# Layer norms of the block preparation moved to ScalarE and GpSimd, with a step table for each engine

## The chip, the cores and the metric

One NeuronCore of a Trainium2 chip runs the whole kernel. The metric is the device time of one execution in microseconds (us); it is given as the median of three runs. Five engines work in parallel and meet only through semaphores: TensorE (PE, matmuls; PEld is its weight load), VectorE (DVE), ScalarE (ACT), GpSimd (POOL) and SyncE (SP), which issues the DMAs.

## The reference

The input x is 8 sequences of 512 tokens with 128 features. One layer is computed, cut here to what matters:

```
xn  = layernorm(x)                                # eps 1e-5
a   = softmax(q k^T / 8) v Wo + bo                # 16 heads of 64, q, k, v from xn
y   = xn + a
x2  = x + (y - mean(y)) * rsqrt(var(y) + 1e-3) * gamma + beta
f   = layernorm(x2)                               # eps 1e-5
s   = sigmoid(f @ router_w.T)                     # 64 experts in 8 groups
coef = top-4 groups, then top-8 experts, normalized, * 2.5     # one row of 64 per token
out = x2 + sum_e coef_e * (silu(f Wg_e) * (f Wu_e)) Wd_e + shared expert(f)
```

The two layer norms that the change is about are the one that gives x2 and the one that gives f.

## The kernel before

**Two phases.** First comes attention, in 64 pairs of heads (8 pairs for each of the 8 sequences), each pair in 4 slots; it ends near 800 us of the span. Then the experts: 8 blocks (one for each sequence of 512 tokens) of 33 tiles. Tile 0 is the shared expert, tiles 1 to 32 are two routed experts each. In both phases the high and low 16-bit halves of the operands are multiplied in three matmuls (`product`, `mm` at L998).

**One tile of the expert phase.** TensorE makes the gate (3 matmuls of 512 columns), the up projection (3), the spread coefficients (1) and the down projection (3). It works four tiles ahead: in its step k it issues gate, up and coefficients of tile k+4 (`gate_up`), then the down projection of tile k (`down`). The gate goes to ScalarE (`silu`, L628), then VectorE multiplies it with the up result (L957, "prod") and that with the coefficients (L963, "hid"), ScalarE takes the high half of it (L633, `hid_hi_tile`) and GpSimd the low half (L497, `hid_lo`). Gate, up and coefficients have two PSUM banks each. So the gate of tile t+2 waits for the silu of tile t, its up projection for the product (L957) of tile t, and its coefficients for the L963 of tile t.

**The preparation of the next block** runs among the tiles of the current one, in numbered steps. The function `route(m, r, k)` of each engine holds its part of step k; before the change step k is placed at tile k on every engine, behind the tile's own work. What is done:

- step 1, VectorE: y = xn + bias (L777); step 2: statistics (`bn_stats`, L781); step 3: mean and variance (`bn_aggr`, L785) and var + eps (L788)
- step 3, GpSimd: the power -0.5 of that (L435); step 2, GpSimd: x + beta (L446)
- step 4, VectorE: (y - mean) * gamma in four instructions (L792); step 6, VectorE: times 1/std, plus x, in four (L800), which gives x2
- steps 7 and 8: the same statistics of x2; step 9, VectorE: (x2 - mean) / std in four (L807), which gives f
- step 8, TensorE: four transposes of f (L1056); step 11, ScalarE, and 12, VectorE (L812): high and low half of the transpose; step 11, TensorE: the logits; step 14, ScalarE: the sigmoid (L563), which needs another activation table, so two table loads stand around it; step 14, GpSimd: scores plus bias (L441)
- steps 16 to 28, VectorE: the choice of groups and experts in small instructions that each read the one before (L822 to L887); step 27, TensorE: the transpose of the coefficients; step 30, ScalarE, and 31, VectorE: their halves

**Block 0** has no block ahead of it. Its preparation is placed by tables (`DVE_0`, `POOL_0`, `ACT_0`, `PE_0`) in the last 8 pairs of attention: slot 0 is slot 0 of pair 56, slot 31 the last slot of pair 63. `ROUTE_0` is 56.

Within an engine the order is as it is written out; nothing is reordered. On VectorE `own` counts an instruction, `settled` waits until all counted ones are done, and `then` does both.

Of the kernel before, what the change touches and what calls it, by code (L numbers as in the profile page):

```python
# [18 lines left out]
P = 128  # L19
# [45 lines left out]
def layer(nc, x, Wq, bq, Wk, bk, Wv, bv, Wo, bo, gamma, beta, router_w, e_bias,  # L65
          Wg, Wu, Wd, SWg, SWu, SWd, out):
    with ExitStack() as ctx:
# [74 lines left out]
        veps, rstd, total, share = (take(QT) for _ in range(4))  # L142
# [85 lines left out]
        xbeta = sem("xbeta")  # L228
        rstd_done = sem("rstd_done")
        c_var = sem("c_var")  # L230
# [161 lines left out]
        def _(pool):  # L392
# [29 lines left out]
            def route(m, r, k):  # L422
# [95 lines left out]
        def _(act):  # L518
# [38 lines left out]
            def route(m, r, k):  # L557
                if k == 11:
                    act.wait_ge(tr_c, m + 1)
                    nc.scalar.activation(fT_hi[r], bank_c(m), ACT.Copy).then_inc(tr_c_hi, 1)  # L560
# [79 lines left out]
            def run_block(n, r, last):  # L640
                for k in range(1, TILES if last else TILES + 1):
# [6 lines left out]
                    if not last:  # L648
                        route(n + 1, 1 - r, k)
# [9 lines left out]
        def _(dve):  # L659
# [92 lines left out]
            def route(m, r, k):  # L752
# [26 lines left out]
                if k in (2, 7):  # L779
                    for t in range(QT):  # L780
                        own(nc.vector.bn_stats(bn[:, t, :], (ya if k == 2 else x2[r])[:, t, :]))  # L781
                    settled()
                if k in (3, 8):
                    for t in range(QT):
                        own(nc.vector.bn_aggr(mean_var[:, t, :], bn[:, t, :]))  # L785
                    settled()
                    eps = POST_EPS if k == 3 else LN_EPS
                    nc.vector.tensor_scalar(veps, mean_var[:, :, 1], eps, None, ALU.add).then_inc(c_var, 1)  # L788

                if k == 4:  # L790
                    for t in range(QT):
                        own(nc.vector.scalar_tensor_tensor(out=ya[:, t, :], in0=ya[:, t, :], scalar=mean_var[:, t, 0:1],  # L792
                                                           in1=gamma_b, op0=ALU.subtract, op1=ALU.mult))
                if k == 6:
                    settled()
                    dve.wait_ge(rstd_done, m * 2 + 1)
                    dve.wait_ge(xbeta, m + 1)
                    wait(dve, out_sent, (m - 1) * 16)
                    for t in range(QT):
                        own(nc.vector.scalar_tensor_tensor(out=x2[r][:, t, :], in0=ya[:, t, :], scalar=rstd[:, t:t + 1],  # L800
                                                           in1=xin[r][:, t, :], op0=ALU.mult, op1=ALU.add))
                    settled()
                if k == 9:
                    dve.wait_ge(rstd_done, m * 2 + 2)
                    wait(dve, tr_c, m)
                    for t in range(QT):
                        last = nc.vector.tensor_scalar(xf[:, t, :], x2[r][:, t, :], mean_var[:, t, 0:1],  # L807
                                                       rstd[:, t:t + 1], ALU.subtract, ALU.mult)
                    last.then_inc(xf_done, 1)
# [167 lines left out]
            def run_block(n, r, last):  # L977
                for k in range(1, TILES if last else TILES + 1):
# [7 lines left out]
                    if not last:  # L986
                        route(n + 1, 1 - r, k)
# [8 lines left out]
        def _(pe):  # L996
# [51 lines left out]
            def route(m, r, k):  # L1048
                if k == 8:
                    pe.wait_ge(xf_done, m + 1)  # L1050
                    if isinstance(m, int) and m == 0:
                        pe.wait_ge(v_lo_done, ROUTE_0 + 3)
# [5 lines left out]
                if k == 11:  # L1058
                    pe.wait_ge(tr_c_lo, m + 1)
                    if isinstance(m, int) and m == 0:  # L1060
                        pe.wait_ge(v_lo_done, ROUTE_0 + 4)
# [219 lines left out]
```

## Time and profile before

| | |
|---|---|
| median of 3 runs (lowest, highest) | 1426.02 us (1425.08, 1428.25) |
| the profiled execution, its own time | 1428.47 us |
| its span, first to last instruction | 1426.7 us |
| TensorE busy (share of the span) | 1358.8 us (95%) |
| VectorE | 1119.4 us (78%) |
| ScalarE | 847.6 us (59%) |
| GpSimd | 888.0 us (62%) |
| granted TensorE clock, mean | 0.997 of full |

The span is what the trace shows between the first and the last instruction; the execution's own time is 1.8 us more. Shares are averages over both phases. TensorE's busy time is modelled from the start of pipelined matmuls, so its idle time is better read from the waits.

### The profile page before, as it was taken

How to read it: one execution, taken by the hardware profiler on the slowest of the kernel's cores; microseconds unless marked ns; L12 is line 12 of the kernel's file. 1: busy time of each engine (PE TensorE's matmuls, PEld its weight loads, DVE VectorE, ACT ScalarE, POOL GpSimd, SP SyncE). 2: the span in 40 equal slices, each digit the busy share in tenths (PEclk: the TensorE clock that was granted, in tenths of full speed). 3: DMA queues.
4: the chain of work that ended last, by engine and by line, in shares of the span. 5: the costliest groups of instructions: out<-in, count | busy, mean ns of one | idle time of the engine just before them, and what ended most of it. 6: DMA issues, size and time to landing. Idle time of an engine off the chain costs nothing.

```text
span 1426.7 us, 35687 instructions
## 1 busy us (share of the span) xinstructions
PE 1358.8 (95%) x12985; PEld 769.2 (54%) x12985; DVE 1119.4 (78%) x2005; ACT 847.6 (59%) x1496; POOL 888.0 (62%) x650
## 2 busy tenths in 40 slices
PE   3799999999999999999998999999989999999998
PEld 1366666666666666666665544344434444343443
DVE  5777777777777877777898888787878787777865
ACT  3566666666666666666666555555546554555554
POOL 3576777777677767767766755555555555555554
PEclk9999999999999999999999999999999999999999
DMA  7233333333333333333322000000000000000000
GB/s 181 52 76 84 78 85 75 82 79 74 79 74 79 74 79 74 83 78 84 86 62 51 9 1 8 8 8 9 2 15 0 15 0 16 0 15 0 1 8 8
DMA packets 84832, 67.45 MB, mean 47 GB/s; under 512 B 27792, under 2 KB 75216, under 8 KB 84688
## 3 DMA queue, kind: packets, MB, share of 16 engines
q1 hardware_dynamic: 84688, 65.52, 18.6%
q8 instruction: 92, 1.51, 0.5%
q14 instruction: 52, 0.43, 0.1%
HBM read 13.05 MB, written 2.10 MB: 11 GB/s over the span
## 4 chain that ended last, share of the span: by engine, by line
PE 63%; issue 19%; DVE 8%; POOL 5%; SPq 2%; ACT 1%; POOLq 0%; DMA 0%; DVEq 0%; ACTq 0%
PE bank L998 61%; POOL arena L497 4%; PE bank L1185 2%; DVE arena L902 1%; DVE arena L957 1%; DVE arena L963 1%; DVE arena L792 1%; POOL arena L462 1%; DVE arena L742 0%; DVE arena L807 0%; POOL arena L435 0%; DMA arena<-arena 0%; DVE arena L922 0%; ACT arena L633 0%; SPq L323 0%
## 5 line engine op out<-in xcount | busy, mean ns | idle before, releaser
L998 PE MATMUL bank<-arena 128*128 128x512 f16 (+5 forms) x12600 | 1328.0, 265 | 52.5 <-DVE arena L957 16.9
L998 PEld LDWEIGHTS bank<-arena 128*128 128x128 f16 (+3 forms) x12600 | 724.7, 98 | 622.0 <-issue 38.0
L462 POOL TENSOR_TENSOR arena<-arena 128x1024 f16<-128x1024 f32 x256 | 484.9, 1895 | 223.8 <-ACT arena L590 220.1
L497 POOL TENSOR_TENSOR arena<-arena 128x512 f16<-128x512 f32 x264 | 307.2, 1165 | 281.5 <-ACT arena L633 278.8
L902 DVE TENSOR_REDUCE arena<-bank 128x2 f32<-128x1024 f32 x256 | 311.8, 1218 | 55.2 <-PE bank L998 51.9
L590 ACT ACTIVATE arena<-bank 128x512 f32<-128x512 f32 x512 | 276.7, 595 | 82.7 <-PE bank L998 82.7
L633 ACT ACTIVATE arena<-arena 128x512 f16<-128x512 f32 x264 | 165.9, 628 | 189.9 <-DVE arena L963 186.5
L957 DVE TENSOR_TENSOR arena<-arena,bank 128x512 f32<-128x512 f32 x256 | 174.9, 683 | 88.8 <-ACT arena L628 59.0
L963 DVE TENSOR_TENSOR arena<-arena,bank 128x512 f32<-128x512 f32 x256 | 175.9, 687 | 29.3 <-DVE arena L957 3.8
L628 ACT ACTIVATE arena<-bank 128x512 f32<-128x512 f32 x264 | 155.5, 589 | 63.3 <-PE bank L998 62.7
L579 ACT ACTIVATE arena<-bank,arena 128x512 f16<-128x512 f32 x128 | 88.0, 688 | 152.8 <-PE bank L998 152.8
L933 DVE SCALAR_TENSOR_TENSOR arena<-bank,arena 128x512 f16<-128x512 f32 x128 | 95.4, 746 | 17.8 <-ACT arena L579 16.4
L939 DVE TENSOR_TENSOR arena<-bank,arena 128x512 f16<-128x512 f32 x64 | 44.2, 691 | 47.3 <-ACT arena L609 47.3
L594 ACT ACTIVATE arena<-bank 2x1024 f16<-2x1024 f32 x64 | 65.0, 1015 | 24.2 <-PE bank L998 24.1
L922 DVE TENSOR_TENSOR arena<-bank,arena 128x256 f32<-128x256 f32 x128 | 54.3, 424 | 4.4
L920 DVE RECIPROCAL arena<-bank 128x4 f32<-128x4 f32 x128 | 23.3, 182 | 35.4 <-PE bank L998 34.2
L615 ACT ACTIVATE arena<-bank 128x512 f16<-128x512 f32 x64 | 37.8, 590 | 11.9 <-PE bank L1185 11.8
L911 DVE TENSOR_TENSOR arena<-bank,arena 128x512 f32 (+1 forms) x64 | 43.6, 681 | 0.0
L928 DVE TENSOR_TENSOR arena<-bank,arena 128x512 f16<-128x512 f32 x64 | 43.5, 680 | 0.0
L1185 PE MATMUL bank<-arena 128*128 128x128 f32 x256 | 39.2, 276 | 2.4 <-DVE arena L911 2.3
L1185 PEld LDWEIGHTS bank<-arena 128*128 128x128 f32 x256 | 31.9, 143 | 15.5 <-DVE arena L911 4.3
L609 ACT ACTIVATE arena<-bank 128x512 f16<-128x512 f32 x64 | 38.4, 600 | 3.0 <-PE bank L998 1.4
(103 smaller groups left out, 416.8 us busy)
## 6 DMA issues: line engine op xcount, KB each, us to landing
arena<-arena SPq DMA_DIRECT2D x384, 128.0 KB, 2.4
arena<-in_L_attn_x SPq DMA_DIRECT2D x9, 256.0 KB, 2.9
arena<-in_L_ffn_Wg SPq DMA_DIRECT2D x32, 64.0 KB, 2.1
arena<-in_L_ffn_Wu SPq DMA_DIRECT2D x32, 64.0 KB, 2.2
arena<-in_L_ffn_Wd SPq DMA_DIRECT2D x32, 64.0 KB, 2.4
out<-arena SPq DMA_DIRECT2D x8, 256.0 KB, 2.3
arena<-in_L_attn_Wq SPq DMA_DIRECT2D x1, 512.0 KB, 4.1
arena<-in_L_attn_Wk SPq DMA_DIRECT2D x1, 512.0 KB, 5.1
```

The source lines that it names most:

```text
L462: pool.tensor_tensor(num_lo[:, u % 2, s, :, :], num[:, u % 2, s, :, :], num_hi[:, u % 2, s, :, :, 1], ALU.subtract).then_inc(lo_pool, 1)
L497: pool.tensor_tensor(hid_lo[:, r, :], hid[:, r, :], hid_hi[:, r, :], ALU.subtract).then_inc(hid_lo_done, 1)
L579: nc.scalar.activation(flat[:, (u + 3) % 2, (ZQH, ZKH)[which], :], ps_proj, ACT.Identity, bias=bias[:, n:n + 1]).then_inc(qk_hi, 1)
L590: nc.scalar.activation(num[:, u % 2, s, h, :], ps_st[ST_BANK[2 * s + h]], ACT.Exp).then_inc(exp_done, 1)
L628: nc.scalar.activation(silu_g[:, r % 3, :], ps_gate[r % 2], ACT.Silu).then_inc(silu_done, 1)
L633: nc.scalar.activation(hid_hi[:, r, :], hid[:, r, :], ACT.Copy).then_inc(hid_hi_done, 1)
L902: nc.vector.tensor_reduce(rmax[:, up % 2, q, :], ps_max2.rearrange("p (h k) -> p h k", h=2), AX.X, ALU.max).then_inc(max_done, 1)
L933: nc.vector.scalar_tensor_tensor(out=flat[:, (u + 3) % 2, (ZQL, ZKL)[s], :], in0=ps_proj, scalar=(bq8, bk_c)[s][:, n:n + 1], in1=flat[:, ( ...
L957: nc.vector.tensor_tensor(prod[:, i % 2, :], silu_g[:, i % 3, :], ps_up[i % 2], ALU.mult).then_inc(prod_done, 1)
L963: nc.vector.tensor_tensor(hid[:, i % 6, :], prod[:, i % 2, :], ps_coef[(k - 1) % 2], ALU.mult).then_inc(hid_done, 1)
L998: return nc.tensor.matmul(out_, lhsT, rhs, start=start, stop=stop, skip_group_check=True)
L1185: last = nc.tensor.transpose(ps_turn[:, k * P:(k + 1) * P], ctxn[:, u % 2, k, :], ident)
```

## The change

Steps 4 and 6 and step 9 leave VectorE:

- VectorE computes in steps 3 and 8 one more small row, the negated mean. GpSimd multiplies it with 1/std ("shift"), so that the norm is y * rstd + shift.
- ScalarE applies scale and shift, four instructions of 128 columns for each norm, in two steps: 4 and 5 for the first norm, 9 and 10 for the second.
- GpSimd multiplies with gamma and adds x + beta (new step 6, two instructions of 128x512). VectorE waits for its result before step 7.

Every engine gets a table for blocks 1 to 7 too (`DVE_N`, `POOL_N`, `ACT_N`, `PE_N`), which says at which tile its steps stand. Steps 16 to 28 of VectorE, before at tiles 16 to 28, now stand at tiles 19 to 28, so that three tiles hold two steps each. On GpSimd the preparation's steps now stand ahead of the tile's own instruction, not behind it.

```diff
-DVE_0 = {0: (1,), 1: (2,), 2: (3,), 3: (4,), 5: (6,), 6: (7,), 7: (8,), 9: (9,), 11: (12,), 19: (16,), 20: (17,),
-         21: (18,), 22: (19, 20), 23: (21,), 24: (22, 23), 25: (24,), 26: (25,), 27: (26,), 28: (27,), 29: (28,), 31: (31,)}
-POOL_0 = {0: (1,), 2: (2,), 3: (3,), 7: (8,), 16: (14,)}
-ACT_0 = {11: (11,), 15: (14,), 31: (30,)}
-PE_0 = {11: (8,), 15: (11,), 31: (27,)}
+DVE_0 = {0: (1,), 1: (2,), 2: (3,), 9: (7,), 10: (8,), 15: (12,), 21: (16,), 22: (17,), 23: (18, 19), 24: (20, 21),
+         25: (22, 23), 26: (24,), 27: (25,), 28: (26,), 29: (27,), 30: (28,), 31: (31,)}
+POOL_0 = {0: (1,), 2: (2,), 3: (3,), 7: (6,), 10: (8,), 20: (14,)}
+ACT_0 = {5: (4,), 6: (5,), 12: (9,), 13: (10,), 15: (11,), 19: (14,), 31: (30,)}
+PE_0 = {15: (8,), 19: (11,), 31: (27,)}
+
+DVE_N = {1: (1,), 2: (2,), 3: (3,), 8: (7,), 9: (8,), 15: (12,), 19: (16,), 20: (17,), 21: (18, 19), 22: (20, 21),
+         23: (22, 23), 24: (24,), 25: (25,), 26: (26,), 27: (27,), 28: (28,), 31: (31,)}
+POOL_N = {2: (2,), 3: (3,), 6: (6,), 9: (8,), 17: (14,)}
+ACT_N = {5: (4,), 6: (5,), 11: (9,), 12: (10,), 14: (11,), 17: (14,), 30: (30,)}
+PE_N = {11: (8,), 14: (11,), 27: (27,)}
...
                 if k in (3, 8):
                     pool.wait_ge(c_var, m * 2 + (1 if k == 3 else 2))
-                    pool.tensor_tensor(rstd, veps, half_pow, ALU.pow).then_inc(rstd_done, 1)
+                    pool.tensor_tensor(rstd, veps, half_pow, ALU.pow).then_inc(rstd_pow, 1)
+                    pool.wait_ge(rstd_pow, m * 2 + (1 if k == 3 else 2))
+                    pool.tensor_tensor(shift, nmean, rstd, ALU.mult).then_inc(rstd_done, 1)
+                if k == 6:
+
+                    pool.wait_ge(scaled, m + 1)
+                    pool.tensor_tensor(ya, ya, gamma_b.unsqueeze(1).broadcast_to([P, QT, D]), ALU.mult).then_inc(gained, 1)
+                    wait(pool, out_sent, (m - 1) * 16)
+                    pool.wait_ge(xbeta, m + 1)
+                    pool.wait_ge(gained, m + 1)
+                    pool.tensor_tensor(x2[r], ya, xin[r], ALU.add).then_inc(x2_done, 1)
...
                 for k in range(1, TILES if last else TILES + 1):
+                    if not last:
+                        for part in POOL_N.get(k, ()):
+                            route(n + 1, 1 - r, part)
                     tile(n * TILES + k, (r * TILES + k) % 6)
-                    if not last:
-                        route(n + 1, 1 - r, k)
...
             def route(m, r, k):
+                if k in (4, 5):
+                    act.wait_ge(rstd_done, m * 2 + 1)
+                    for t in ((0, 1) if k == 4 else (2, 3)):
+                        last = nc.scalar.activation(ya[:, t, :], ya[:, t, :], ACT.Identity,
+                                                    bias=shift[:, t:t + 1], scale=rstd[:, t:t + 1])
+                    if k == 5:
+                        last.then_inc(scaled, 1)
...
                 if k in (2, 7):
+                    if k == 7:
+                        dve.wait_ge(x2_done, m + 1)
...
+                    then(nc.vector.tensor_scalar(nmean, mean_var[:, :, 0], -1.0, None, ALU.mult))
...
-                if k == 4:
-                    for t in range(QT):
-                        own(nc.vector.scalar_tensor_tensor(out=ya[:, t, :], in0=ya[:, t, :], scalar=mean_var[:, t, 0:1],
-                                                           in1=gamma_b, op0=ALU.subtract, op1=ALU.mult))
-                if k == 6:
-                    settled()
-                    dve.wait_ge(rstd_done, m * 2 + 1)
...
-                if k == 9:
-                    dve.wait_ge(rstd_done, m * 2 + 2)
```

ScalarE's steps 9 and 10 read x2 and write f in the same form as 4 and 5. TensorE's two points of block 0 at which attention yields its bank to the preparation move one pair later.

## Rows read from the trace of the kernel before

**Rows 1.** Busy time by engine in stretches; x counts instructions

```profile
1079.00:1111.02 32.02, 32.02 (x150) 14.43 (x150) 28.02 (x67) 17.54 (x30) 19.02 (x17) 1.00 0.00 1
1124.47:1143.71 19.24, 16.83 (x75) 6.49 (x72) 16.80 (x40) 7.81 (x14) 10.63 (x10) 1.00 0.04 14
720.00:740.00 20.00, 17.33 (x239) 11.55 (x236) 19.18 (x37) 11.15 (x20) 13.77 (x9) 1.00 0.30 74
```

**Rows 2.** Waits of PE, 815 to 1340 us: us in total, times, longest

```profile
PE bank L998 <- DVE arena L957: 16.9, 17, 1.6
```

**Rows 3.** Timeline of PE at the head of a block: start, us

```profile
1135.00 7.12 PE L998 MATMUL bank<-arena 128*128 128x512 f16 x30 [0.83 <-DVE arena L957]
1143.71 1.85 PE L998 MATMUL bank<-arena 128*128 128x512 f16 x7 [1.59 <-DVE arena L957]
```

**Rows 4.** Timeline of DVE at that head, steps 4, 6 and 9

```profile
1127.73 1.13 DVE L792 SCALAR_TENSOR_TENSOR arena<-arena 128x128 f32<-128x128 f32 x4
1131.60 2.47 DVE L800 SCALAR_TENSOR_TENSOR arena<-arena 128x128 f32<-128x128 f32 x4
1134.26 0.69 DVE L957 TENSOR_TENSOR arena<-arena,bank 128x512 f32<-128x512 f32 x1 [0.19 <-DVE arena L800]
1141.12 1.94 DVE L807 TENSOR_SCALAR arena<-arena 128x128 f32<-128x128 f32 x4 [0.91 <-POOL arena L435]
```

**Rows 5.** Timeline of POOL beside them

```profile
1132.50 1.16 POOL L497 TENSOR_TENSOR arena<-arena 128x512 f16<-128x512 f32 x1 [0.33 <-ACT arena L633]
1141.06 1.16 POOL L497 TENSOR_TENSOR arena<-arena 128x512 f16<-128x512 f32 x1
```

**Rows 6.** Timeline of ACT in the routing steps, two silus

```profile
1090.12 0.60 ACT L628 ACTIVATE arena<-bank 128x512 f32<-128x512 f32 x1 [0.21 <-PE bank L998]
1092.28 0.60 ACT L628 ACTIVATE arena<-bank 128x512 f32<-128x512 f32 x1 [0.29 <-PE bank L998]
```

**Rows 7.** Timeline of DVE there: products of tiles 17, 20, 22, 24 to 26, 29, 30

```profile
1082.01 0.67 DVE L957 TENSOR_TENSOR arena<-arena,bank 128x512 f32<-128x512 f32 x1
1087.75 0.69 DVE L957 TENSOR_TENSOR arena<-arena,bank 128x512 f32<-128x512 f32 x1
1092.03 0.68 DVE L957 TENSOR_TENSOR arena<-arena,bank 128x512 f32<-128x512 f32 x1
1096.08 0.69 DVE L957 TENSOR_TENSOR arena<-arena,bank 128x512 f32<-128x512 f32 x1 [0.19 <-DVE arena L861]
1098.28 0.69 DVE L957 TENSOR_TENSOR arena<-arena,bank 128x512 f32<-128x512 f32 x1 [0.19 <-DVE arena L866]
1100.75 0.69 DVE L957 TENSOR_TENSOR arena<-arena,bank 128x512 f32<-128x512 f32 x1 [0.19 <-DVE arena L870]
1106.81 0.68 DVE L957 TENSOR_TENSOR arena<-arena,bank 128x512 f32<-128x512 f32 x1
1108.21 0.68 DVE L957 TENSOR_TENSOR arena<-arena,bank 128x512 f32<-128x512 f32 x1
```

**Rows 8.** Timeline of DVE and POOL around step 20

```profile
1089.16 0.42 DVE L846 TENSOR_TENSOR arena<-arena 128x256 f32<-128x256 f32 x1
1089.50 0.42 DVE L847 TENSOR_TENSOR arena<-arena 128x256 f32<-128x256 f32 x1
1089.98 1.16 POOL L497 TENSOR_TENSOR arena<-arena 128x512 f16<-128x512 f32 x1 [0.77 <-ACT arena L633]
```

**Rows 9.** Groups by line: busy us, mean ns

```profile
L446 POOL TENSOR_TENSOR arena<-arena 128x512 f32<-128x512 f32 x8 | 10.2, 1276 | 0.0
L435 POOL TENSOR_TENSOR arena<-arena 128x4 f32<-128x4 f32 x16 | 16.3, 1016 | 3.5 <-DVE arena L788 2.8
L579 ACT ACTIVATE arena<-bank,arena 128x512 f16<-128x512 f32 x128 | 88.0, 688 | 152.8 <-PE bank L998 152.8
L563 ACT ACTIVATE arena<-bank 128x256 f32<-128x256 f32 x8 | 3.1, 384 | 1.9 <-PE bank L998 1.9
L563 ACT ACT_TABLE_LOAD x8 | 10.3, 1283 | 0.1
```

More of the change, by code:

```diff
@@ L141, in layer @@
         bn, mean_var = tiles4(take(QT * 6)), tiles4(take(QT * 2))
-        veps, rstd, total, share = (take(QT) for _ in range(4))
+        veps, rstd, total, share, nmean, shift = (take(QT) for _ in range(6))
         tri = take(G * G)
@@ L228, in layer @@
         xbeta = sem("xbeta")
+        rstd_pow = sem("rstd_pow")
         rstd_done = sem("rstd_done")
+        scaled = sem("scaled")
+        gained = sem("gained")
+        x2_done = sem("x2_done")
         c_var = sem("c_var")
@@ L557, in route @@
             def route(m, r, k):
+                if k in (4, 5):
[5 more added lines that the diff above has]
+                        last.then_inc(scaled, 1)
+                if k in (9, 10):
+                    act.wait_ge(rstd_done, m * 2 + 2)
+                    for t in ((0, 1) if k == 9 else (2, 3)):
+                        last = nc.scalar.activation(xf[:, t, :], x2[r][:, t, :], ACT.Identity,
+                                                    bias=shift[:, t:t + 1], scale=rstd[:, t:t + 1])
+                    if k == 10:
+                        last.then_inc(xf_done, 1)
                 if k == 11:
@@ L648, in run_block @@
                     if not last:
-                        route(n + 1, 1 - r, k)
+                        for part in ACT_N.get(k, ()):
+                            route(n + 1, 1 - r, part)
                 if last:
@@ L786, in route @@
                     settled()
+                    then(nc.vector.tensor_scalar(nmean, mean_var[:, :, 0], -1.0, None, ALU.mult))
                     eps = POST_EPS if k == 3 else LN_EPS
                     nc.vector.tensor_scalar(veps, mean_var[:, :, 1], eps, None, ALU.add).then_inc(c_var, 1)
-                if k == 4:
-                    for t in range(QT):
-                        own(nc.vector.scalar_tensor_tensor(out=ya[:, t, :], in0=ya[:, t, :], scalar=mean_var[:, t, 0:1],
-                                                           in1=gamma_b, op0=ALU.subtract, op1=ALU.mult))
-                if k == 6:
-                    settled()
-                    dve.wait_ge(rstd_done, m * 2 + 1)
[L797 to L802, printed above, removed]
-                if k == 9:
-                    dve.wait_ge(rstd_done, m * 2 + 2)
[L805 to L809, printed above, removed]
                 if k == 12:
@@ L986, in run_block @@
                     if not last:
-                        route(n + 1, 1 - r, k)
+                        for part in DVE_N.get(k, ()):
+                            route(n + 1, 1 - r, part)
             tail(run, ((PAIRS, 0),))
@@ L1051, in route @@
                     if isinstance(m, int) and m == 0:
-                        pe.wait_ge(v_lo_done, ROUTE_0 + 3)
+                        pe.wait_ge(v_lo_done, ROUTE_0 + 4)
                     if isinstance(m, int) and m == 1:
@@ L1060, in route @@
                     if isinstance(m, int) and m == 0:
-                        pe.wait_ge(v_lo_done, ROUTE_0 + 4)
+                        pe.wait_ge(v_lo_done, ROUTE_0 + 5)
                     for t in range(QT):
@@ L1157, in run @@
                                 wait(pe, qk_lo, 2 * t)
-                            if p == ROUTE_0 + 3:
+                            if p == ROUTE_0 + 4:
                                 pe.wait_ge(tr_c_lo, 1)
-                            if p == ROUTE_0 + 4:
-                                pe.wait_ge(sigm, 1)
                         else:
@@ L1167, in run @@
                         pe.wait_ge(qk_lo, upto(2 * t + 2, 2 * PAIRS))
+                        if p == ROUTE_0 + 5:
+                            pe.wait_ge(sigm, 1)
                         for k in range(QT):
@@ L1221, in run_block @@
                     if not last:
-                        route(n + 1, 1 - r, k)
+                        for part in PE_N.get(k, ()):
+                            route(n + 1, 1 - r, part)
                 transpose_sum(n)
@@ L1253 @@
 TURN_AT = {(-1, 0): (1,), (-1, 1): (2, 3), (-1, 2): (4, 5), (-1, 3): (6, 7)}
-ROUTE_COUNT = {1: 1, 2: QT, 3: QT, 4: QT, 6: QT, 7: QT, 8: QT, 16: 2, 17: 4, 18: 3, 19: 2,
+ROUTE_COUNT = {1: 1, 2: QT, 3: QT + 1, 7: QT, 8: QT + 1, 16: 2, 17: 4, 18: 3, 19: 2,
                20: 2, 21: 2, 22: 2, 23: 1, 24: QT, 25: QT, 26: 2, 27: 3, 28: 0}
```

## The prediction

> **What bounds the kernel now.** I began with the busy shares of the whole run: TensorE 95%, VectorE 78%, the others near 60%. Such a mean hides two regimes of the expert phase, so I cut it into stretches. Where VectorE chooses the experts, TensorE has no idle time at all in 32.02 us [rows 1]. At the head of a block, where the layer norms stand, it is busy for 16.83 of 19.24 us [rows 1]: 2.41 us idle. The waits of TensorE name the cause: over six and a half blocks nearly all of it, 16.9 us in 17 waits, is for the product L957 of VectorE [rows 2]. The timeline has two such waits in each head, 0.83 and 1.59 us [rows 3], and VectorE's own timeline shows what it did just before: step 6 (L800) for 2.47 us, and step 9 (L807), for which it waited 0.91 us on GpSimd's power and then worked 1.94 us [rows 4]. So at a head the end is set by VectorE, elsewhere by TensorE. TensorE's clock is granted in full in every stretch [rows 1].
>
> **The slack of VectorE.** ScalarE's silus, when they wait for TensorE, come 2.16 us apart [rows 6]: a tile of ten matmuls of 0.216 us. The up projection of tile t+2 starts 17 matmuls after that of tile t has ended, 3.67 us. The product takes 0.69 and some 0.11 for two semaphores. So the product may start 3.67 - 0.80 = 2.87 us late without cost; each later microsecond is idle time of TensorE. VectorE needs 1.40 us for a bare tile (1106.81 to 1108.21) [rows 7], so it catches up 0.76 us a tile where it has nothing else.
>
> **What is removed.** In each head 1.13 + 2.47 + 1.94 = 5.5 us of VectorE and its wait of 0.91 [rows 4]. That is more than both waits of TensorE, so the question is what is late next.
> - VectorE keeps the statistics and gets two rows of 4 elements, the negated mean; by instructions of that size about 0.2 us each. Tile 4 then starts about 2.4 us late, as now (2.6), and from there VectorE has bare tiles up to 7. Nothing reaches 2.87.
> - ScalarE: an activation of 128 columns. 256 columns take 384 ns [rows 9], 512 take 600 [rows 6], so 128 some 280; a bias read from a tile costs about 0.09 (688 against 0.60 us) [rows 9, 6], and I take the same for the scale: 0.46, overlapped by some 0.09, so 0.8 us for a step of two. With silu and high half (0.6 + 0.63) that is 2.0 us in tiles 5, 6, 11 and 12, under 2.16. It takes away ScalarE's idle time and no more. Bounds: 0.6 to 1.1 us a step; at 1.1 ScalarE is 0.2 late a tile, inside the slack.
> - GpSimd: two instructions like L446, 2 x 1.28 us, and the small product of 4 elements behind the power of 1.02 [rows 9]. I take 0.3 for it; the power itself is the upper bound, an idle instruction (0.1) the lower. Behind them on its queue stand the low halves of tiles 6 and 9, due four tiles later in TensorE's order (`down` of tile k follows the gate of k+4); 3 to 4 us late they still arrive. x2 is ready about when VectorE ends tile 8, where it waits for it; I reckon from 0.6 us early to 1.5 late, and that is slack too.
> - The transposes move from TensorE's step 8 to 11, one that has already asked for the silu of tile 13, which is behind ScalarE's part at tile 12. No wait.
>
> So the head's waits go: -16.5 us (16.9 less some 0.4 that stand elsewhere). Bounds: -16.9 to -12, if one short wait stays.
>
> In block 0, VectorE is busy for 19.18 of 20 us around the same steps and TensorE idle 2.67 [rows 1]. I take -2.0 of it, and +0.5 because its later steps stand one slot later, where attention runs out: -1.5, bounds -4 and +3.
>
> **What is pressed together.** Steps 16 to 28 keep their end at tile 28 but start three tiles later. Everything from the logits to step 17 is shifted as a whole, so I take the lateness over from the trace. The silu at 1090.12 [rows 6] is of tile 22, it starts 0.06 after its gate; the up projection is done 0.65 later, so the product could have started at 1090.77 and did at 1092.03 [rows 7]: late 1.26. Five tiles back it could have at 1079.97 and did at 1082.01: late 2.04 at tile 17, left over from the sigmoid's table loads. Before, this melts. After, the same 2.04 stands at tile 20, and then:
> - tiles 20, 21 (steps 17, 18 + 19): before, 5.74 us for three tiles (1082.01 to 1087.75) [rows 7]. One bare tile less: 4.34 against 4.32 of TensorE. Late 2.06.
> - tile 22 (20 + 21): 4.28 for two before, 2.88 now, 0.10 more because step 21 waits at once for step 20: 2.98 against 2.16. Late 2.88.
> - tile 23 (22 + 23): 4.05 for two, now 2.65. Late 3.37.
> - tile 24: 2.20, tile 25: 2.47 [rows 7]. Late 3.72, the peak; then it falls.
>
> 3.72 - 2.87 = 0.85 us of new idle time per block.
>
> **The collision in tile 22.** Step 6 of before is four alike instructions, each with two SBUF inputs. L792, the same shape, took 1.13 us for four; L800 took 2.47, and beside it GpSimd's L497 ran from 1132.50 for 1.16 us [rows 4, 5]. Likewise L807, begun at 1141.12 behind an L497 that began at 1141.06. So such an instruction of VectorE stands still while GpSimd's runs. Step 20 begins at 1089.16, its second instruction at 1089.50 ends at 1089.92, and GpSimd begins its low half at 1089.98 [rows 8], 0.82 after step 20 began: its time is set by VectorE's L963 and ScalarE's high half. Before, VectorE was then at L957, which reads PSUM and runs through. Now step 21 starts at 0.79, is followed by a dependent one, and one of the two must stand for GpSimd's 1.16. So tile 22 takes 4.14, and the idle time per block is 0.85 + 1.16 = 2.01 us. In the Trainium skill, "SBUF — State Buffer", section "Who interferes with whom", the same is stated: a VectorE instruction with two SBUF inputs contends with a GpSimd instruction that reads SBUF, and whoever starts first holds the port for its whole instruction. By that rule, the trace agrees. The rule also speaks against moving gamma and residual to GpSimd, but beside those two VectorE has only L957 and L963, each with one PSUM input.
>
> Seven preparations: 7 x 2.01 = +14.1 us. (The first of them is in block 0, beside the rest of attention; it is counted like the others.)
>
> **Sum.** -16.5 - 1.5 + 14.1 = -3.9 us. Against the profiled execution's 1428.47 us (span 1426.7) that is 1424.6; its time lies 2.45 over the median of the runs shown, so in terms of the median 1426.02 the forecast is 1422.1 us.
>
> **The rivals.**
> - *No collision, or one that is absorbed.* If GpSimd begins its low half later (ScalarE held up by a silu), step 21 slips through. For it: the two meet within 0.03 us. Against: with either first, the second of the dependent pair is still in the way. Time: +0.85 x 7 = 6 instead of 14.1, so 1426.0 - 12.0 = 1414.
> - *More collisions; slower.* In tile 21 the last instruction of step 19 begins about 0.63 after step 18, in tile 23 step 23 about 0.65 after step 22; GpSimd comes at 0.82. If GpSimd were 0.2 us earlier or VectorE 0.2 later, each stands for 1.16 more. The same can happen in step 16, whose first instructions stood in GpSimd's way already. It decides from one further collision per block on: 1422.1 + 8.1 = 1430.2, two 1438.3. For it: the distances are under 0.2 us. Against: they come from rows that repeat alike in each block.
> - *The change doesn't do what it says at the head: table loads.* If Identity isn't in the table that silu uses, each of ScalarE's four visits brings two loads of 1.28 [rows 9]: 4.6 us for tiles 5, 6, 11 and 12, 4.9 late in each pair, 5.6 us idle per block beyond the slack, so 1461. Against: Copy stands between silus without a load, and Identity with a bias between exponentials (L579). No run here shows Identity beside silu; the Trainium skill, "ScalarE: Activation LUTs", section "Table sets: the hidden batching unit", says that cheap functions such as identity are in every set, and by it there would be no load.
>
> **Chances.** Forecast 0.42, with a range of its own of 1417 to 1427; no collision 0.27; more collisions 0.23; table loads 0.03; 0.05 for what I don't see (x2 or f so late that TensorE waits). 0.2%, 2.85 us, is about what a measurement tells from no change: under 1423.2 is faster. Of the forecast's 0.42 some 0.25 lie there, 0.12 within and 0.05 above. Faster 0.25 + 0.27 = 0.52; same 0.12 + 0.05 = 0.17; slower 0.31. The range goes from 1411, below the second case, to 1433, above one further collision; two collisions and the loads are left out.
>
> **What would show it.** After the change no wait of TensorE for L957 between tiles 4 and 14; waits of about 2 us in sum at tiles 24 to 27 of each block, for L957; one of step 21's instructions at about 1.6 us instead of 0.42, beside an L497. No ACT_TABLE_LOAD but the two around the sigmoid. VectorE's busy time down by some 5 us a block less the collision. The prediction fails if waits remain at the head (then ScalarE or GpSimd is late, and their L numbers stand in the wait) or if steps 16 to 28 pass without a wait.

## The result: 1413.63 us, and the profile after

| | before | after |
|---|---|---|
| median (lowest, highest), first comparison | 1425.70 us (1425.08, 1428.25) | 1413.63 us (1413.28, 1419.42) |
| ratio, 95% interval | | 0.9912 [0.9897, 0.9927] |
| median, second comparison (`c1_after_again`) | 1427.80 us (1426.22, 1429.16) | 1417.79 us (1415.60, 1420.36) |
| ratio, 95% interval | | 0.9927 [0.9913, 0.9940] |
| profiled execution | 1428.47 us | 1419.42 us, span 1417.7, clock 0.995 |

The change is faster by 12.1 us in the first comparison and 10.0 in the second, under 1%, and both intervals lie clear of no change; forecast were 3.9. The time lies in the range, 8.5 us under the predicted one.

**How to compare the two.** A window of fixed length is a poor ruler, since the steps stand at other tiles now. TensorE's own transposes are better: the sum transposes end a block, the f transposes and the coefficient transposes stand in its middle. Between two of them the number of tiles is known, a tile is ten matmuls, and the unbroken run below shows what a matmul takes: 23.91 us for 110, 0.216 each and 0.16 for the end of the last. What is over is lost time. In the timeline of TensorE after the change, one head:

```profile
1120.59 0.60 PE L1230 MATMUL bank<-arena 128*128 128x128 f32 x4
1121.02 23.91 PE L1019 MATMUL bank<-arena 128*128 128x512 f16 x110
1144.77 0.60 PE L1077 MATMUL bank<-arena 128*128 128x128 f32 x4
```

and the same stretch before, of which [rows 3] show the two listed waits:

```profile
1124.03 0.60 PE L1209 MATMUL bank<-arena 128*128 128x128 f32 x4
1124.47 9.71 PE L998 MATMUL bank<-arena 128*128 128x512 f16 x43
...
1145.40 0.60 PE L1056 MATMUL bank<-arena 128*128 128x128 f32 x4
```

After: 110 matmuls in one unbroken run, 24.18 us for 11 tiles, 23.76 + 0.42 for the transposes: nothing lost. Before: 21.37 us for 80 matmuls, 17.28 + 0.44: 3.65 us lost. The two waits listed there come to 2.42. The other 1.23 stand in no list. A wait is counted from the end of a matmul's record, which lasts 0.379 us where the next could start after 0.216; that is 0.33 for the two. The other 0.9 are gaps of 0.09 to 0.15 us inside the runs (43 matmuls are 9.29 us and took 9.71; the 30 of [rows 3] are 6.48 and took 7.12).

The whole expert phase by this ruler, from the first coefficient transposes to the last sum transposes, tiles that changed sides taken out:

| stretch | before | after | difference |
|---|---|---|---|
| head of block 0, first coefficient to f transposes (after: three tiles more, 6.48 us) | 34.25 us | 38.40 us | -2.3 |
| lost in the six other heads, each | 3.4 to 3.9 | 0.0 | -22.3 in sum |
| lost from the resumption after the sigmoid to the coefficient transposes, each of seven | 0.22 (block 0: 0.57) | 2.16 (block 0: 1.01) | +12.1 in sum |
| lost at the end of two blocks, in sum | 4.27 | 4.40 | +0.1 |
| sum, and measured over the phase | 621.76 | 609.34 | -12.4 |

The last row but one is no work of the change: in two of the seven blocks every kernel here, the one before too, loses about 2 us or more behind the coefficient transposes. After the change VectorE stands there for 3 us, and the profile shows nothing that it waits for:

```profile
1039.36 0.69 DVE L977 TENSOR_TENSOR arena<-arena,bank 128x512 f32<-128x512 f32 x1 [3.17 <-issue]
```

The cause stays open.

TensorE's waits from 815 to 1330 us, after the change (us in total, times, longest); they answer to [rows 2]:

```profile
PE bank L1019 <- DVE arena L977: 6.7, 15, 0.7
PE bank L1019 <- ACT arena L674: 1.9, 2, 0.9
PE bank L1019 <- ACT arena L664: 1.6, 7, 0.2
```

L977 is the product, L957 before: 16.9 us have become 6.7. None of it is at a head; 5.8 are in the routing and 0.9 at those two block ends. The page's busy times:

```profile
PE 1359.0 (96%) x12985; PEld 771.3 (54%) x12985; DVE 1086.9 (77%) x1925; ACT 865.9 (61%) x1560; POOL 910.1 (64%) x682
```

VectorE's is down by 32.5 us, 4.1 for each of eight preparations. What does the scaling now is in ScalarE's timeline:

```profile
971.98 0.86 ACT L583 ACTIVATE arena<-arena 128x128 f32<-128x128 f32 x2
972.75 0.57 ACT L664 ACTIVATE arena<-bank 128x512 f32<-128x512 f32 x1
```

and in GpSimd's:

```profile
969.90 1.02 POOL L446 TENSOR_TENSOR arena<-arena 128x4 f32<-128x4 f32 x1 [2.39 <-DVE arena L828]
971.00 0.20 POOL L448 TENSOR_TENSOR arena<-arena 128x4 f32<-128x4 f32 x1
975.03 1.27 POOL L452 TENSOR_TENSOR arena<-arena 128x512 f32<-128x512 f32 x1
976.48 1.27 POOL L456 TENSOR_TENSOR arena<-arena 128x512 f32<-128x512 f32 x1 [0.17 <-POOL arena L452]
```

ScalarE's step is 0.86 us (forecast 0.8), the shift on GpSimd 0.20 (0.3), gamma and residual 1.27 each (1.28), and the silu L664 follows ScalarE's Identity with no table load between (the page counts 8 loads at the sigmoid and 8 at the silu, as before). Now the routing. VectorE's timeline at tiles 21 and 22:

```profile
1009.76 0.69 DVE L977 TENSOR_TENSOR arena<-arena,bank 128x512 f32<-128x512 f32 x1
...
1011.18 0.42 DVE L866 TENSOR_TENSOR arena<-arena 128x256 f32<-128x256 f32 x1
1011.51 0.42 DVE L867 TENSOR_TENSOR arena<-arena 128x256 f32<-128x256 f32 x1
1011.97 0.42 DVE L872 TENSOR_TENSOR arena<-arena 128x256 f32<-128x256 f32 x1
1012.43 1.26 DVE L873 TENSOR_TENSOR arena<-arena 128x256 f32<-128x256 f32 x1
1013.61 0.67 DVE L977 TENSOR_TENSOR arena<-arena,bank 128x512 f32<-128x512 f32 x1
```

GpSimd's timeline there, with the low half:

```profile
1012.00 1.40 POOL L518 TENSOR_TENSOR arena<-arena 128x512 f16<-128x512 f32 x1 [1.08 <-ACT arena L669]
```

and TensorE's:

```profile
1014.34 2.50 PE L1019 MATMUL bank<-arena 128*128 128x512 f16 x10 [0.70 <-DVE arena L977]
1017.04 3.14 PE L1019 MATMUL bank<-arena 128*128 128x512 f16 x13 [0.20 <-DVE arena L977]
```

The collision is there, and it is alike in all seven blocks: L872 begins 0.03 us ahead of the low half and slips through, L873 (the same instruction by shape, 0.42 us) takes 1.26 beside it. From product to product tile 22 is 3.85 us; forecast were 4.14. Two listed waits of TensorE follow, 0.90 us of the 2.16 that the stretch loses; the rest is short gaps again.

### The profile page after: what moved, and what is told of

The parts are those of the page before. It is cut to its first block, busy times and chain, and to the rows that moved or that the text cites. A ratio compares the mean times of both kernels' runs of the same rounds, so it can differ in the third digit from the quotient of the medians.

```text
span 1417.7 us, 35701 instructions
## 1 busy us (share of the span) xinstructions
PE 1359.0 (96%) x12985; PEld 771.3 (54%) x12985; DVE 1086.9 (77%) x1925; ACT 865.9 (61%) x1560; POOL 910.1 (64%) x682
## 4 chain that ended last, share of the span: by engine, by line
PE 74%; DVE 9%; issue 9%; POOL 4%; ACT 2%; SPq 2%; DVEq 0%; DMA 0%; POOLq 0%; ACTq 0%
PE bank L1019 72%; POOL arena L518 3%; DVE arena L977 2%; PE bank L1206 2%; DVE arena L922 1%; POOL arena L483 1%; DVE arena L983 1%; ACT arena L664 1%; DVE arena L779 0%; SPq L334 0%; SPq L339 0%; DVE arena L757 0%; DVE arena L842 0%; SPq L333 0%; DVE arena L942 0%
## 5 line engine op out<-in xcount | busy, mean ns | idle before, releaser
L977 DVE TENSOR_TENSOR arena<-arena,bank 128x512 f32<-128x512 f32 x256 | 175.4, 685 | 113.3 <-ACT arena L664 67.9
L664 ACT ACTIVATE arena<-bank 128x512 f32<-128x512 f32 x264 | 155.1, 588 | 63.6 <-PE bank L1019 58.1
```

What stands on the lines that cost most here:

```text
L664: nc.scalar.activation(silu_g[:, r % 3, :], ps_gate[r % 2], ACT.Silu).then_inc(silu_done, 1)
L977: nc.vector.tensor_tensor(prod[:, i % 2, :], silu_g[:, i % 3, :], ps_up[i % 2], ALU.mult).then_inc(prod_done, 1)
```

## The experiments

Line numbers differ a little from kernel to kernel; the operation and the tile name say which instruction it is. "Lost" is always by the ruler above. Different comparisons were run on different chips, so across them the ratios to the kernel before say more than the medians.

**Where do the 2.16 us in the routing come from?** Two experiments. `r1_spread` gives steps 20 and 21 tiles of their own and moves what follows by one:

```diff
-DVE_N = {..., 21: (18, 19), 22: (20, 21), 23: (22, 23), 24: (24,), 25: (25,), 26: (26,), 27: (27,), 28: (28,), 31: (31,)}
-ACT_N = {..., 30: (30,)}
-PE_N = {11: (8,), 14: (11,), 27: (27,)}
+DVE_N = {..., 21: (18, 19), 22: (20,), 23: (21,), 24: (22, 23), 25: (24,), 26: (25,), 27: (26,), 28: (27,), 29: (28,), 32: (31,)}
+ACT_N = {..., 31: (30,)}
+PE_N = {11: (8,), 14: (11,), 28: (27,)}
```

TensorE's wait for the coefficients moves to its step 28 with them. `r3_short22` takes the collision away and leaves the table alone; in tile 22 GpSimd computes only 4 of the 512 columns of the low half (the other 508 are left out):

```diff
+                if k == 22 and not last:
+                    pool.tensor_tensor(hid_lo[:, r, 0:4], hid[:, r, 0:4], hid_hi[:, r, 0:4],
+                                       ALU.subtract).then_inc(hid_lo_done, 1)
+                    return
```

> The changed kernel, with steps 20 and 21 at two tiles (22 and 23); the steps behind them, the transpose of the coefficients and their halves stand one tile later. Theory A: of the 28.08 us from the silu wait after the sigmoid to the coefficient transposes, 2.16 us are idle time of TensorE, made by the pairs of steps (lateness over the slack) and the collision in tile 22. Then it takes 28.08 us for 13 tiles instead of 12, at most 0.3 us idle, no step 21 instruction over 0.5 us, and the run is 7 x 1.9 = 13 us faster than the changed kernel: about 1400.5 us. Theory B: the idle time there is left over from the sigmoid's table loads and only moved with them; spreading the steps changes less than 3 us: 1411 to 1414.

> The changed kernel; in tile 22 GpSimd subtracts only 4 of 512 columns of the low half, the other 508 are left out. Theory A (collision): step 21's last instruction falls from 1.26 us to 0.42 (the first stays), tile 22 from 3.85 to 3.0 us, TensorE's idle time in the routing stretch by 0.84 a block: 1413.6 - 5.9 = 1407.7 us. Theory B (only the number of VectorE's instructions counts, the long one is slow for another reason): the instruction stays at 1.26 and the time at 1413.6.

Measured: `r1_spread` 1413.20 us (before on that chip 1428.04), ratio 0.9891 [0.9866, 0.9916]; `r3_short22` 1410.05 (forecast 1407.7), ratio 0.9874 [0.9850, 0.9898]. In `r1_spread` VectorE's timeline has L873 back at its own duration:

```profile
1011.70 0.42 DVE L872 TENSOR_TENSOR arena<-arena 128x256 f32<-128x256 f32 x1
1012.15 0.42 DVE L873 TENSOR_TENSOR arena<-arena 128x256 f32<-128x256 f32 x1
1012.50 0.68 DVE L977 TENSOR_TENSOR arena<-arena,bank 128x512 f32<-128x512 f32 x1
```

and TensorE waits for the product 1.7 us instead of 6.7 in all of 815 to 1330; both waits that are left stand at the two block ends, none in the routing:

```profile
PE bank L1019 <- DVE arena L977: 1.7, 2, 1.0
PE bank L1019 <- ACT arena L664: 1.6, 7, 0.2
PE bank L1019 <- DVE arena L903: 0.9, 5, 0.2
```

Lost to the coefficient transposes are 0.44 us instead of 2.16, and 0.35 more behind them: 1.37 us less in four of the blocks. It is less in the others: 0.6 in block 0, whose routing had lost only 1.01, and 1.0 in the two with the block ends, which lose 0.7 more there now. Over the phase that makes 8.1 us (601.20 instead of 609.34). In `r3_short22` the same stretch falls from 28.08 to 27.24 us: the collision costs 0.84 per block, which is exactly what L873 stood still (1.26 - 0.42). So the pressing together costs 2.16 - 0.22 = 1.94 us a block. 0.84 of it is the collision, which `r3_short22` shows by itself; the other 1.10 is the difference, and `r1_spread`, which takes one of three pairs apart, shows that about half of it goes with that pair (1.37 - 0.84). The medians follow only in part: `r1_spread` missed its 1400.5 by 12.7 us and lies at the rival's number (1411 to 1414). That is taken up below.

**Which of the two norms was the head?** Four experiments put VectorE's instructions back. `r4_second_dve` only those of the second norm (step 9, at tile 11), `r5_first_dve` only those of the first (steps 4 and 6, at tiles 4 and 6, gamma and residual with them), `r6_both_dve` both (steps 4, 6 and 9 at tiles 5, 7 and 11), `r10_both_order` the same with GpSimd's preparation behind the tile's low half. The core of `r5_first_dve`:

```diff
-DVE_N = {1: (1,), 2: (2,), 3: (3,), 8: (7,), ...
+DVE_N = {1: (1,), 2: (2,), 3: (3,), 4: (4,), 6: (6,), 8: (7,), ...
...
+                if k == 4:
+                    for t in range(QT):
+                        own(nc.vector.scalar_tensor_tensor(out=ya[:, t, :], in0=ya[:, t, :], scalar=mean_var[:, t, 0:1],
+                                                           in1=gamma_b, op0=ALU.subtract, op1=ALU.mult))
...
```

> The changed kernel with the second norm's four scaling instructions (step 9) back on VectorE, at tile 11 (block 0: slot 13), and away from ScalarE. Theory A: what cost time before was that steps 4, 6 and 9 and the wait for the power stood close together; at tile 11 VectorE has been on time since tile 7, so 1.94 us plus a possible wait stay under the slack of 2.87: 1413.6 us within 1. Theory B: the removal from VectorE itself is worth its share of the 3.7 us a block at the head, 1.6 or more for step 9: 1413.6 + 11 = 1425 us.

> The changed kernel with all scaling back on VectorE as before the change (steps 4, 6, 9), placed at tiles 5, 7 and 11; GpSimd has no gamma and no residual. Theory A (placement): lateness 2.4 at tile 4, 2.0 at tile 6, 2.9 to 3.0 at tile 8, some 3.4 behind steps 7 and 8 at tile 10: 0.5 to 0.8 us idle a block at the head, so 1413.6 + 5 = 1418.5 us. Theory B (the engine): the head's 3.7 us a block come back whole beside the routing's 2 us: 1413.6 + 25 = 1439 us.

> The first norm's scaling alone is back on VectorE (steps 4 and 6 at tiles 4 and 6), the second norm's stays on ScalarE. Theory A (what the head gained comes from the first norm; the VectorE instructions with two SBUF inputs meet GpSimd's low halves): the head, sum transposes to f transposes, costs 3 us more than after, 27 instead of 24.2, and the time is 1413.5 + 7 x 3 + about 2 in attention = 1437. Rival B (each norm gives half; the loss comes from the second norm landing on a late VectorE): head 25.5, time 1425.

> Both norms back on VectorE as in r6_both_dve, and GpSimd's preparation behind the tile's own low half. Theory A (in r6 the low halves that queue up behind power and shift were what VectorE's scaling instructions ran into): the head falls from r6's 27.5 to about 25.5 for 11 tiles, the time from 1440.6 by 7 x 2 = 14 to 1427. Rival B (the collisions are there in either order): 1440.

| | median us | ratio, interval | head (11 tiles), us | lost |
|---|---|---|---|---|
| after | 1413.63 | 0.9912 [0.9897, 0.9927] | 24.18 | 0.0 |
| `r4_second_dve` | 1421.78 | 0.9949 [0.9928, 0.9969] | 24.18 | 0.0 |
| `r5_first_dve` | 1437.94 | 1.0084 [1.0067, 1.0101] | 27.05 to 27.14 | 2.9 |
| `r6_both_dve` | 1440.60 | 1.0087 [1.0068, 1.0106] | 27.44 to 27.54 | 3.3 |
| `r10_both_order` | 1447.74 | 1.0145 [1.0128, 1.0162] | 27.78 to 28.30 | 3.6 to 4.1 |

The head's gain hangs on the first norm: put back by itself it costs 2.9 us a head, the second by itself nothing, and the second beside the first 0.4 more. `r5_first_dve` came out at its forecast of 1437. VectorE's timeline of `r5_first_dve` shows both its steps at more than twice the 1.13 us that L792 had [rows 4]:

```profile
974.89 2.84 DVE L818 SCALAR_TENSOR_TENSOR arena<-arena 128x128 f32<-128x128 f32 x4
...
980.47 2.47 DVE L826 SCALAR_TENSOR_TENSOR arena<-arena 128x128 f32<-128x128 f32 x4
```

GpSimd's timeline of the same kernel shows what ran beside them, two low halves and then one:

```profile
974.73 2.33 POOL L518 TENSOR_TENSOR arena<-arena 128x512 f16<-128x512 f32 x2
979.88 1.16 POOL L518 TENSOR_TENSOR arena<-arena 128x512 f16<-128x512 f32 x1 [2.82 <-ACT arena L669]
```

and TensorE waits after each:

```profile
978.39 4.66 PE L1031 MATMUL bank<-arena 128*128 128x512 f16 x20 [1.46 <-DVE arena L989]
983.87 14.80 PE L1031 MATMUL bank<-arena 128*128 128x512 f16 x67 [0.83 <-DVE arena L989]
```

In `r4_second_dve` step 9 collides as well, and costs nothing in the blocks: 2.45 us at a VectorE that was in time stays under the slack of 2.87 that the prediction worked out:

```profile
987.01 2.45 DVE L834 TENSOR_SCALAR arena<-arena 128x128 f32<-128x128 f32 x4
```

The median of `r4_second_dve` is nevertheless 8 us over the changed kernel's first and over its forecast of 1413.6, with blocks that are the same to 0.02 us. What is lost lies ahead of them. In 700 to 760 us, where attention keeps VectorE full, TensorE is busy for 55.34 us (56.46 in after's profile), and the step 9 of block 0 stands in that stretch: 1.1 us. That they belong together is argued, not shown. Much of the rest goes with the granted clock: its five runs had a mean of 0.991 to 0.998, and at equal clock they took 1.4 to 2.7 us more than those of `c1_after_again` (1418.15 against 1415.60 at 0.998), on another chip.

`r6_both_dve` was to come out at 1418.5 by my theory of that time, that the head is a matter of placement alone: if steps 4, 6 and 9 get distance from each other, VectorE may keep them. It came out at 1440.60, 22 us above that and at its rival's number (1439); that theory fell. The next one, that the low halves which queue up behind power and shift are what those steps run into, and that the old order on GpSimd would undo it, fell too: `r10_both_order` was to gain 14 us and lost 7. VectorE's timeline in it:

```profile
984.40 2.49 DVE L818 SCALAR_TENSOR_TENSOR arena<-arena 128x128 f32<-128x128 f32 x4
...
989.63 2.49 DVE L826 SCALAR_TENSOR_TENSOR arena<-arena 128x128 f32<-128x128 f32 x4
...
999.80 2.42 DVE L846 TENSOR_SCALAR arena<-arena 128x128 f32<-128x128 f32 x4
```

Three collisions in either order, in six of the seven blocks (2.54, 2.49 and 2.57 us in `r6_both_dve`). A low half falls due in every tile, and a VectorE step of four such instructions in the same tile mostly meets it. Not always: in the kernel before, step 4 passed in 1.13 [rows 4], and in the block 0 of these two runs steps 4 and 6 took 1.13 to 1.38. There `r6_both_dve` needed only 0.3 us more than the changed kernel from the first coefficient transposes to the f transposes (38.70 against 38.40), `r5_first_dve`, whose two collided there too (2.48 and 2.05), 1.1 more. That speaks for the collisions as the larger part of what the first norm costs on VectorE; no run has its instructions in the other heads without them, so the shares of collision and bare work stay open. What the old order costs beyond that, 0.3 to 0.8 us per head, I can't name.

**Does the order on GpSimd matter for the changed kernel?** `r7_pool_order`:

```diff
                 for k in range(1, TILES if last else TILES + 1):
+                    tile(n * TILES + k, (r * TILES + k) % 6)
                     if not last:
                         for part in POOL_N.get(k, ()):
                             route(n + 1, 1 - r, part)
-                    tile(n * TILES + k, (r * TILES + k) % 6)
```

> GpSimd's preparation stands behind the tile's own low half, as it did before the change, in blocks 1 to 7. Theory A (with the scaling on ScalarE nothing of VectorE at the head has two SBUF inputs but the statistics, so the order of GpSimd is without effect): 1413.5 within 2. Rival B (gamma and residual end a low half later, VectorE waits 1.2 us more for x2 at tile 8, beyond its slack): up to 7 x 1.2 = +8, so 1421.

Measured 1421.95 us, ratio 0.9971 [0.9957, 0.9985]: the rival's number. VectorE's statistics of x2 now wait, which they do not in after:

```profile
978.62 0.87 DVE L820 BATCH_NORM_STATS2 arena<-arena 128x6 f32<-128x128 f32 x4 [1.59 <-POOL arena L456]
```

The six heads lose 0.1 to 0.6 us, six routings 0.13 more than in after, and block 0 alone 2.4 (1.2 up to its f transposes, 1.2 in its routing): span from the first coefficient transposes to the end 618.6 us instead of 613.5. That is 5.1 of the 8.3 us. The rest fits the clock: its three runs at 0.998 took 1418.6 to 1420.7, 3 to 5 us more than `c1_after_again` at that clock, on another chip. The order of the two on GpSimd is a working part of the change, for which the prediction had no term.

**Where do the medians lose what the blocks gain?** The profiled execution of after has this at the end of attention (columns: us; busy time and count of TensorE, its weight load, VectorE, ScalarE, GpSimd; granted clock; DMA share; GB/s):

```profile
795.00:800.00 5.00, 1.95 (x34) 1.27 (x32) 4.90 (x7) 1.11 (x3) 5.00 (x3) 0.98 0.00 2
800.00:805.00 5.00, 5.00 (x56) 3.74 (x55) 1.91 (x6) 1.92 (x4) 3.47 (x3) 0.68 0.02 3
```

TensorE stands for 3 of 5 us (in the last 9 us ahead of the coefficient transposes it is busy for 5.95, in the kernel before for 7.45), and in the next 5 the granted clock is 0.68, which means that for most of it the lower of its two levels was granted. VectorE's timeline ahead of it has two instructions of 256 columns, which take 0.29 and 0.42 us in the later blocks:

```profile
792.62 3.68 DVE L894 TENSOR_SCALAR arena<-arena 128x256 f32<-128x256 f32 x1
796.33 1.99 DVE L895 TENSOR_TENSOR arena<-arena 128x256 f32<-128x256 f32 x1
```

and GpSimd's has the cast of the selectors, begun 0.07 us earlier:

```profile
792.55 3.60 POOL L474 CAST arena<-arena 128x4096 f16<-128x4096 f32 x1
```

`r8_split_cast` splits the cast in four:

```diff
-                pool.tensor_copy(spread.rearrange("p t (e n) -> p (t e) n", e=2),
-                                 twice.unsqueeze(2).broadcast_to([P, E, EXPERT])).then_inc(spread_done, 1)
+                for q in range(4):
+                    es = slice(q * E // 4, (q + 1) * E // 4)
+                    last = pool.tensor_copy(spread.rearrange("p t (e n) -> p (t e) n", e=2)[:, es, :],
+                                            twice[:, es].unsqueeze(2).broadcast_to([P, E // 4, EXPERT]))
+                last.then_inc(spread_done, 1)
```

> The cast of the selectors at the end of attention, one GpSimd instruction of 3.60 us, is four of a quarter each. Theory A (VectorE's instruction beside it stands still for 3.68 us, TensorE runs dry at 795 to 800 us of the span and its clock then falls): VectorE stands for 1 us at most, TensorE is busy 3 us or more of 795 to 800, no clock below 0.9 at 800 to 805, the time falls by 2 to 5 us, to 1408.5 to 1411.5. Rival B (the dip has another cause, or the four pieces block just as long together): 1413.5 within 1.5.

Measured 1413.98 us, ratio 0.9914 [0.9898, 0.9931]. Its trace does what theory A says:

```profile
788.70 1.12 DVE L897 TENSOR_SCALAR arena<-arena 128x256 f32<-128x256 f32 x1
789.86 1.13 DVE L898 TENSOR_TENSOR arena<-arena 128x256 f32<-128x256 f32 x1
```

Everything stands earlier here: the first coefficient transposes come at 796.93 us. In the 9 us ahead of them TensorE is busy for 7.39 instead of 5.95, and the clock stays at 1.00. The median does not move by anything that can be measured: it is the rival's number, and theory A's 1408.5 to 1411.5 was missed. So the last three runs put the changed kernel and both edits on one chip:

> The changed kernel itself, on one chip with the two below. Its run-to-run range follows the granted clock: in four runs 1413.3 us came with a mean clock of 0.999 to 1.000 and 1419.4 with 0.995. Theory A (the difference is the clock, which dips after idle stretches at the start and the end of attention): 1413 to 1415 where the clock is 0.998 or more, some 0.8 us longer per 0.001 below. Rival B (the chip of the first comparison was a lucky one): 1416 or more at a full clock.

> r1_spread beside the changed kernel on one chip. Theory A (its blocks are 1.4 us shorter, and in its first comparison it lost part of that to a clock of 0.991 to 0.996): at equal clock 6 to 9 us under the changed kernel, and 1 to 9 in the medians. Rival B (the gain of the blocks is given back somewhere in every run): the medians within 1.5 us of each other at equal clock.

> r1_spread with the selectors' cast in four pieces. Theory A (the routing's idle time and the idle stretch at the end of attention are two separate costs): 2.5 us under r1_spread at equal clock, 1404 to 1409, the best of all. Rival B (the end of attention is set by other work, as r8_split_cast's median of 1413.98 suggests): equal to r1_spread within 1 us.

| one chip; before 1427.80 | median us | ratio, interval | the one run at a mean clock of 0.998 |
|---|---|---|---|
| after (`c1_after_again`) | 1417.79 | 0.9927 [0.9913, 0.9940] | 1415.60 |
| `c2_spread_again` | 1408.34 | 0.9867 [0.9850, 0.9884] | 1405.95 |
| `r9_spread_split` | 1406.90 | 0.9857 [0.9842, 0.9872] | 1406.39 |

Theory A on the spread holds: the medians are 9.5 us apart, the two runs at equal clock 9.7, a little more than the 6 to 9 that it had forecast. The profiles show 7.7 of it behind the first coefficient transposes (601.09 us instead of 608.82); the rest was not located. In the first comparison of `r1_spread` the gain was largely hidden by the clock: its runs had a mean of 0.991 to 0.996, the changed kernel's 0.995 to 1.000, and the kernel before took 2.3 us longer on that chip. How much the clock weighs is best read from the ten runs of `r7_pool_order`: three at 0.991 took 1425.3 to 1426.4 us, three at 0.998 took 1418.6 to 1420.7, 0.85 us per 0.001. At 0.998 the changed kernel took 1415.60, between theory A of `c1_after_again` (1413 to 1415) and its rival (1416 or more), so a difference between the chips is neither shown nor excluded.

For the split cast the question stays open. By the medians the rival holds. At equal clock the two runs at 0.998 are 0.4 us apart, against the split; but `r8_split_cast` took 1412.18 at 0.999 where the changed kernel, in another comparison, took 1413.34 and 1413.92, and `r9_spread_split` at 0.995 and 0.996 lies 1 to 2.3 us under what `c2_spread_again` would take there by a line through its own runs (an estimate). A gain of 1 to 1.5 us, which is what TensorE stands less at the end of attention (7.39 - 5.95), is possible and not shown; theory A of `r8_split_cast` had forecast 2 to 5. The runs of `r9_spread_split` lie closer together (1406.4 to 1408.1, against 1405.9 to 1412.5); four and five runs don't show that this is more than chance. `r9_spread_split` and `c2_spread_again` both beat the kernel before and the changed one; the two are not told apart.

## Why the prediction came out as it did

- **Which regime, which engine: right.** At the heads VectorE had set the end, and with its scaling gone TensorE does not wait there at all.
- **The head, -16.5: the term that was mis-sized.** Measured: -22.3 in the six whole heads and -2.3 in the first, -24.6 in sum. The step that failed is the reading of the loss from the list of waits and the busy time (2.41 idle of 19.24, 16.9 us in 17 waits). The list has 14.4 us for the six heads and 1.9 for the first; it leaves out the short gaps inside a run of matmuls and the 0.16 us by which each record outlasts the next start, 1.23 us in the head shown above. The busy time hides them too: in the prediction's own window 43 and 30 matmuls start [rows 3], 73 of 0.216 are 15.77 us, so 3.47 were lost and not 2.41. (The 75 of [rows 1] count two more that only reach into the window.) The bounds of the term, -16.9 to -12, shut the true value out.
- **What is late next: nothing, right.** ScalarE's steps, the shift, gamma and residual came within 0.1 us of their estimates, no table was loaded, and x2 was there 0.2 us ahead of VectorE's statistics. That was close: `r7_pool_order` shows that with one low half more in front VectorE waits 1.59 us.
- **The routing, +14.1: right in mechanism and size.** 1.94 us a block against 2.01, +12.1 in sum, because block 0's routing lost only 0.45 more than before. The split between the two causes was somewhat off: the collision costs 0.84 instead of 1.16, since L873 began 0.43 us into the low half and stood only for what was left of it, and the pressing together 1.10 instead of 0.85.
- **The collision: right**, to the instruction. Its wording is too narrow: it speaks of two SBUF inputs, but L807, and L894 in block 0, are TENSOR_SCALARs with one tensor input and stood as well (2.45 us in `r4_second_dve`, 3.68 instead of 0.29 in after). The measured time lies beside that of the rival without a collision (1414), and that is chance: the rival's mechanism did not happen.
- **Block 0, -1.5: not resolved.** The first coefficient transposes came at 804.24 us instead of 800.86 in the profiled execution, with clock dips to 0.50 and 0.68 in 5 us slices on the way, and at 805.66 in `c1_after_again`; at 800.27 in `r3_short22`, whose attention phase is that of the changed kernel and had no dip after 50 us. The kernel before had dips too (0.66 in 780 to 785). So -0.6 to +4.8, by the clock; the upper end lies past the bound of +3.
- **The sum.** -24.6 + 12.1 - 0.6 = -13.1 with few dips, against -12.1 and -10.0 measured; the error of the forecast is the head.

## What to carry to other kernels

Read what a bound engine loses from the distance between two fixed points and the count of its instructions times the duration of one; the waits say who is late, not how much is lost. Whether a collision costs is decided by the slack behind it: one step of 2.45 us was free at an engine that was in time, and two of them (2.84 and 2.47) that stood two tiles apart cost 2.9 us a block. Where instructions of two engines collide once per tile, shifting them by a tile or two bought nothing in these runs; moving one side to an engine that stays out of it took the loss away. Steps that are pressed together to make room can give half of that back, so they deserve a table of their own: here taking one pair of three apart was worth 7.7 us in the traces and 9.5 in the medians. And where the clock moves a time by 0.85 us per 0.001, compare runs at equal clock before a difference of a few us is explained.

## What the hardware showed beyond that

- In the ten profiles of the changed kernel and its variants that leave the cast of the selectors whole, TensorE stood for about 3 us at the end of attention. In nine of them the granted clock was at the lower of its two levels right after, for some 3 us (7 in `r5_first_dve`, where it began during the standstill): 0.66 to 0.68 over 5 us in after, `r1_spread`, `r6_both_dve` and `r7_pool_order`. In the tenth, `r3_short22`, TensorE stood as long (busy 5.94 of 9 us, after 5.95) and the clock stayed at 1.00. In the two with the split cast (7.39 of 9) it stayed at 1.00. So such a standstill mostly brought a dip and did not have to. Dips come and go between executions elsewhere too: the changed kernel had 0.83 at 50 to 60 us of the span in one profile and 0.64 in another. In the ten runs of `r7_pool_order` 5.9 us of a range of 7.8 go with the mean clock.
- A VectorE instruction that begins 0.07 us after a long one on GpSimd stands for all of it, 3.68 us beside a cast of 3.60. The same work in four casts takes GpSimd 4.24 us and lets VectorE through after 1.12.
- In each of the seven blocks of the changed kernel an instruction of VectorE (L872) that began 0.03 to 0.04 us before GpSimd's ran at its full speed of 0.42, and GpSimd's took 1.40 us instead of 1.16.
